# State space powers as two 64x64 blocks, and attention's value matmuls in two sets of 256 columns

## What is computed

```python
# layer 0, attention: 16 heads of 16 channels
attn = (einsum('bhqc,bhkc->bhqk', q1, k_eff1) + einsum('bhqc,bhkc->bhqk', q2, k_eff2)) * scale
attn = softmax(attn, axis=-1)
out = einsum('bhqk,bhkd->bhqd', attn, v)
...
# layer 1, state space: D_ = 256 channels, state of N_ = 16
def step(h, x_t):
    h = einsum('dnm,bdm->bdn', A, h) + Bm[None] * x_t[..., None]
    y_t = einsum('dn,bdn->bd', Cm, h) + Dm * x_t
    return (h, y_t)
_, y = scan(step, h0, swapaxes(x, 0, 1))      # x: layernormed
y = gelu(layernorm(y, ln_w, ln_b)) @ W_out.T + b_out
```

## Time and profile before

| | |
|---|---|
| median of 3 runs | 1903.34 us (1901.82 to 1905.7) |
| the profiled execution's own time | 1897.99 us |
| its span, first to last instruction | 1895.5 us |
| PE busy | 1633.4 us (86%) |
| DVE busy | 1215.1 us (64%) |
| ACT busy | 984.4 us (52%) |
| POOL busy | 431.2 us (23%) |
| mean granted TensorE clock | 0.926 |

### The profile page before, as it was taken

One profiled execution on the slowest core, in us unless ns is written; L12 is line 12 of the kernel. 1 busy time (PEld: TensorE's weight loads), 2 busy tenths in 40 slices (PEclk: granted clock), 3 DMA queues, 4 the chain that ended last, 5 costly groups with the idle time before them and its releaser, 6 DMA issues. The chain is left out here.

```text
span 1895.5 us, 33280 instructions
## 1 busy us (share of the span) xinstructions
PE 1633.4 (86%) x10504; PEld 1102.0 (58%) x10506; DVE 1215.1 (64%) x2121; ACT 984.4 (52%) x2005; POOL 431.2 (23%) x568
## 2 busy tenths in 40 slices
PE   5949999999999999988699958999888279999990
PEld 4824333333333333327588847989874169888880
DVE  6649999999999999602688686555465832222224
ACT  3412888888888888870444323434232135555442
POOL 3027000000000000000012145212122245565550
PEclk9955999999999999997799988999898589999995
DMA  5662233334443323000100021131306722222117
GB/s 194 208 176 35 41 40 53 42 52 62 56 67 41 53 41 53 19 9 17 12 1 0 1 57 46 46 89 45 90 1 200 244 87 66 66 64 66 62 65 271
DMA packets 117577, 134.55 MB, mean 71 GB/s; under 512 B 27028, under 2 KB 91560, under 8 KB 117352
## 3 DMA queue, kind: packets, MB, share of 16 engines
q1 hardware_dynamic: 104712, 107.60, 25.0%
q0 software_dynamic: 7584, 20.72, 3.4%
q10 hardware_dynamic: 5184, 4.98, 0.8%
HBM read 92.23 MB, written 36.04 MB: 68 GB/s over the span
## 5 line engine op out<-in xcount | busy, mean ns | idle before, releaser
L1845 DVE TENSOR_REDUCE mx<-ps 128x1 f32<-128x1024 f32 x512 | 602.1, 1218 | 56.7 <-PE ps L1967 56.2
L1884 ACT ACTIVATE PR<-ps 128x512 f32<-128x512 f32 x1024 | 533.1, 604 | 170.9 <-PE ps L2006 170.8
L1967 PE MATMUL ps<-KQ 48*128 48x512 f32 x1024 | 420.1, 488 | 28.5 <-PEq L238 21.7
L2006 PE MATMUL ps<-KQ 50*128 50x512 f32 x1024 | 375.2, 445 | 25.2 <-ACT PR L1884 10.7
L2006 PEld LDWEIGHTS ps<-KQ 50*128 50x128 f32 x1024 | 170.7, 185 | 329.9 <-ACT PR L1884 303.0
L1991 PE MATMUL ps<-PR,VO 128*32 128x512 f32 x2048 | 273.6, 606 | 2.1
L1967 PEld LDWEIGHTS ps<-KQ 48*128 48x128 f32 x1024 | 176.8, 196 | 80.0 <-DVE mx L1845 43.1
L1737 PEld LDWEIGHTS ps<-e_xinT,e_w 128*128 128x128 f32 x1264 | 154.8, 193 | 5.7 <-issue 1.7
L1727 PE MATMUL ps<-eW,e_hiddenT 128*128 x632 | 155.0, 388 | 3.4 <-issue 0.9
L1737 PE MATMUL ps<-e_xinT,e_w 128*128 128x128 f32 x1264 | 155.5, 277 | 1.1 <-ACT e_xinT L1669 1.1
L1697 DVE TENSOR_TENSOR e_y<-ps,b2b 128x256 f32<-128x256 f32 x79 | 33.6, 425 | 172.7 <-DMA expert_outputs<-e_y,e_y_index 163.6
(11 more groups left out here) (274 smaller groups left out, 2212.3 us busy)
## 6 DMA issues: line engine op xcount, KB each, us to landing
KQ<-qk_parts SPq DMA_DIRECT2D x192, 128.0 KB, 6.0
qk_parts<-parts SPq DMA_DIRECT2D x8, 2048.0 KB, 6.9
TB<-toeplitz_lines SPq DMA_DIRECT2D x32, 512.0 KB, 5.8
eW<-in_L_ffn_W SPq DMA_DIRECT2D x16, 512.0 KB, 6.9
eW<-in_L_ffn_W SPq DMA_DIRECT2D x8, 1024.0 KB, 12.0
e_got<-expert_outputs SPq DMA_DIRECT2D x16, 512.0 KB, 10.2
X<-in_L_attn_x SPq DMA_DIRECT2D x8, 512.0 KB, 4.8
V<-OT SPq DMA_DIRECT2D x64, 64.0 KB, 6.8
```

The costliest lines, as they stand in the source:

```text
L1845: nc.vector.tensor_reduce(mx[:, u % RING, h * QT + q:h * QT + q + 1], ps[:, b:b + 2].rearrange("p a n -> p (a n)"), AX, ALU.max, negate=Tr ...
L1884: nc.scalar.activation(PR[:, kt % 2, h], ps[:, st_bank(u, s)], ACT.Exp).then_inc(exp_done, 1)
L1967: made = nc.tensor.matmul(ps[:, max_bank(u, t) + k], kq[half(h, KROWS), 1, h % HR, q * P:(q + 1) * P], kq[half(h, KROWS), 0, h % HR, k * B ...
L2006: nc.tensor.matmul(ps[:, st_bank(u, s)], kq[half(h, AROWS), 0, h % HR, kt * P:(kt + 1) * P], kq[half(h, AROWS), 1, h % HR, qc * BANK:(qc + ...
```

## The change

In the state space stage the power is no longer kept as a 128x128 matrix with zeros off the two diagonal 64x64 blocks, but as those two blocks one above the other, 64 columns wide (`BLK`). Each former matmul of `level` becomes two of 64 rows by 64 columns: `blocks` gives the row ranges 0 to 63 and 64 to 127, and each reads and writes its own range, in the same PSUM bank. They move 64 + 2^l columns. The transposes of W1's power become matmuls with the identity, two blocks each. The last three powers go to a tile `PT` of their own, and `L1137` is split in two blocks too. DVE's and ACT's copies of the power move half as many columns. `build` uses a narrower mask. The matmuls `L1125`, `L1149`, `L1159`, `L1161`, `L1196` and `L1201` stay as they are. PE's loop over the batches is written out; the other engines keep theirs.

In attention `weigh` takes a part: part 0 moves query columns 0 to 255 for the four heads and is issued after the second block of a step, part 1 moves columns 256 to 511 after the fourth. The waits stand before part 0, the signal `pv_done` behind part 1.

```diff
-GT_, OB_, PT1_ = range(3)
-KEPT = PT1_ + len(REACH)
+GT_, OB_ = range(2)
+KEPT = 2
+BLK = P // 2
+BC = BLK // N
...
-            W1 = sbuf(s0, "W1", [P, SLOT, 2 * P])
-            W2 = sbuf(s0, "W2", [P, SLOT, 2 * P])
+            W1 = sbuf(s0, "W1", [P, SLOT, P + BLK])
+            W2 = sbuf(s0, "W2", [P, SLOT, P + BLK])
...
             KM = sbuf(s0, "KM", [P, 2, SLOT, KEPT, P])
+            PT = sbuf(s0, "PT", [P, 2, SLOT, len(REACH), BLK])
+            mask4 = sbuf(s0, "mask4", [P, BC])
...
-                    body((2 * i + 2, 0), (2 * i + 1, 1))
+                if written_out:
+                    for b in range(1, NB - 1):
+                        body((b, b % 2), (b - 1, 1 - b % 2))
+                else:
+                    with eng.Fori(0, (NB - 2) // 2) as i:
+                        body((2 * i + 1, 1), (2 * i, 0))
+                        body((2 * i + 2, 0), (2 * i + 1, 1))
...
                                             pattern=[[N, GC]], channel_multiplier=-1).then_inc(mask_ready, 1)
+                    pool.wait_ge(mask_ready, 1)
+                    nc.gpsimd.tensor_tensor(mask4[:], mask[:, 0:BC], mask[:, BC:GC], op=ALU.add).then_inc(mask_ready, 1)
...
-                        nc.vector.tensor_tensor(W1[:, :, P:2 * P].rearrange("p s (c n) -> p s c n", n=N),
-                                                vA[:, these, :].unsqueeze(2).broadcast_to([P, SLOT, GC, N]),
-                                                spread.unsqueeze(3).broadcast_to([P, SLOT, GC, N]), op=ALU.mult)
+                        nc.vector.tensor_tensor(W1[:, :, P:P + BLK].rearrange("p s (c n) -> p s c n", n=N),
+                                                vA[:, these, :].unsqueeze(2).broadcast_to([P, SLOT, BC, N]),
+                                                mask4[:].unsqueeze(1).unsqueeze(3).broadcast_to([P, SLOT, BC, N]), op=ALU.mult)
...
-                                nc.vector.tensor_copy(dst[:, :, P:2 * P], src[:, :, o:o + P]).then_inc(w1r[h], 1)
+                                nc.vector.tensor_copy(dst[:, :, P:P + BLK], src[:, :, o:o + BLK]).then_inc(w1r[h], 1)
...
-                                last = nc.scalar.copy(of_pair(KM[:, z], h)[:, :, PT1_ + l - LEVELS + 1], src[:, :, o:o + P])
+                                last = nc.scalar.copy(of_pair(PT[:, z], h)[:, :, l - LEVELS + 1], src[:, :, o:o + BLK])
                             if l <= LEVELS:
-                                last = nc.scalar.copy(dst[:, :, P:2 * P], src[:, :, o:o + P])
+                                last = nc.scalar.copy(dst[:, :, P:P + BLK], src[:, :, o:o + BLK])
...
-                                last = nc.tensor.matmul(scan(d)[:, j], KM[:, z, j, PT1_ + k], by_batch(hs[:, j:j + 1])[:, 0, :, 0:TPB - 1 - d],
-                                                        start=True, stop=True, skip_group_check=True)
+                                for r in blocks:
+                                    last = nc.tensor.matmul(scan(d)[r, j], PT[r, z, j, k], by_batch(hs[r, j:j + 1])[:, 0, :, 0:TPB - 1 - d],
+                                                            start=True, stop=True, skip_group_check=True)
...
-                                    nc.tensor.matmul(pair(0, h)[:, s % HS, 0:c + P], W2[:, s, P:2 * P], W1[:, s, P - c:2 * P], start=True, stop=True, skip_group_check=True)
-                                last = nc.tensor.matmul(pair(1, h)[:, s % HS, 0:c + P], W1[:, s, P:2 * P], W2[:, s, P - c:2 * P], start=True, stop=True, skip_group_check=True)
+                                    for r in blocks:
+                                        nc.tensor.matmul(pair(0, h)[r, s % HS, 0:c + BLK], W2[r, s, P:P + BLK], W1[r, s, P - c:P + BLK], start=True, stop=True, skip_group_check=True)
+                                for r in blocks:
+                                    last = nc.tensor.matmul(pair(1, h)[r, s % HS, 0:c + BLK], W1[r, s, P:P + BLK], W2[r, s, P - c:P + BLK], start=True, stop=True, skip_group_check=True)
...
-                                    last = nc.tensor.transpose(pair(1, h)[:, s % HS, 0:P], W1[:, s, P:2 * P], ident[:])
+                                    for r in blocks:
+                                        last = nc.tensor.matmul(pair(1, h)[r, s % HS, 0:BLK], W1[r, s, P:P + BLK], ident[r, r], start=True, stop=True, skip_group_check=True)
...
-                    batches(pe, body)
...
+    WPARTS = 2
+    PART = BANK // WPARTS
...
-            def weigh(u, step):
+            def weigh(u, step, part):
 
                 kt = step % KT
-                pe.wait_ge(exp_done, BLOCKS * u + HG * (step + 1))
-                if step == 0:
-                    pe.wait_ge(vo_ready, u + 1)
-                if kt == 0 and STEPS * u + step > 0:
-                    pe.wait_ge(ot_kept, 2 * u + step // KT)
+                if part == 0:
+                    pe.wait_ge(exp_done, BLOCKS * u + HG * (step + 1))
+                    if step == 0:
+                        pe.wait_ge(vo_ready, u + 1)
+                    if kt == 0 and STEPS * u + step > 0:
+                        pe.wait_ge(ot_kept, 2 * u + step // KT)
+                cols = slice(part * PART, (part + 1) * PART)
                 for h in range(HG):
-                    last = nc.tensor.matmul(ps[2 * HD * h:2 * HD * (h + 1), OT_BANK], VO[:, u % 2, kt, h], PR[:, kt % 2, h],
-                                            start=(kt == 0), stop=(kt == KT - 1))
-                last.then_inc(pv_done, 1)
+                    last = nc.tensor.matmul(ps[2 * HD * h:2 * HD * (h + 1), OT_BANK, cols], VO[:, u % 2, kt, h], PR[:, kt % 2, h, cols],
+                                            start=(kt == 0 and part == 0), stop=(kt == KT - 1), skip_group_check=True)
+                if part == WPARTS - 1:
...
-                    if h == HG - 1 and STEPS * u + step > 0:
-                        weigh(u if step > 0 else u - 1, (step - 1) % STEPS)
-            weigh(UNITS - 1, STEPS - 1)
+                    if h % (HG // WPARTS) == HG // WPARTS - 1 and STEPS * u + step > 0:
+                        weigh(u if step > 0 else u - 1, (step - 1) % STEPS, h // (HG // WPARTS))
+            for part in range(WPARTS):
+                weigh(UNITS - 1, STEPS - 1, part)
```

More of the change, by code:

```diff
@@ L849, in ssm @@
             slots = lambda h: range(HS * h, HS * h + HS)
+            blocks = [slice(BLK * y, BLK * (y + 1)) for y in range(P // BLK)]
             of_pair = lambda t, h: t[:, HS * h:HS * h + HS]
@@ L1214, in body @@
                             pe.wait_ge(small_kept, 2)
-                    batches(pe, body)
+                    batches(pe, body, written_out=True)
         ssm_output(nc, sem, sbuf, ps, X, Y, ident, woT, lnwb, turned)
```

9 lines of the change are left out of this document (4 added, 5 removed).

## The result

The changed kernel takes 1852.84 us (median of 4 runs, 1844.43 to 1859.64), the kernel before 1902.71 (4 runs, 1901.82 to 1905.7): a ratio of 0.9738, 95% interval 0.9708 to 0.9767. It is 50 us faster, inside the range, and 14 us slower than forecast.

What follows compares the result with a forecast made beforehand. Attention was taken as bound by PE's order, state space by PE's columns (DVE at levels 0 and 1). 1898.0 - 12 (attention) - 52 (state space) = 1834 profiled, 5.3 more for the median: 1839; range 1818 to 1858, 1872 with half overlap.

Steps and rivals of the forecast that it cites:

- the attention term: Attention: shorter steps less the copy-step wait gain 0.7 to 0.8 us in each of 16 units, 12 us.
- State space, 52 us: State space stage: seven batches gain 49 us, batch 0 gains 2, the last lone recurrence 1.
- The table: State space batch piece by piece, assuming full block overlap: 30.75 us before, 23.7 after.
- the blocks do not overlap: State space rival: blocks sharing a PSUM bank run singly; stage loses 6 us, attention gains 12: 1897 us, chance 0.08.
- Half overlap, 1864: State space rival: only some 3.5 us of the 7 per batch are gained, 1864 us, chance 0.08.
- Attention's step, 2.46: Attention: PE becomes the bound of a normal step at 2 x (0.66 + 0.57) = 2.46 us, 0.14 to 0.15 less.
- after 16 x 2.46 + 2 x 0.99 = 41.3: Attention unit after the change: sixteen steps plus two waits for ACT's copy, 41.3 us against 42.0 before.
- attention gains nothing: Attention rival: changes of layout cost 0.57 + 0.03 and more, so no gain there: 1851 us, chance 0.14.
- The stall itself: Attention, twice a unit: part 0, due at 0.66, waits 0.99 us for ACT's copy (`ot_kept`), later work queued behind.
- Without that stall it would gain 44: Attention: without the copy-step wait the stage would gain 44 us instead of 12.
- the clock falls in the batches: State space rival: PE at half the clock makes a batch 41 us, not 30.75; 1963 us, chance 0.03.
- The parts costed at nothing: PE's written-out loop, masks on POOL and narrower `build`: no cost, being behind PE's queue or before a waiting transposition.

Runs made afterwards that it cites:

- e6: Changed kernel, in each half level all matmuls of the upper 64x64 block issued first, then all of the lower: 1896.12 us (one run).
- e1: Kernel before with only attention's two half sets of value matmuls (`weigh`), old state space stage: 1903.34 us, ratio 1.0012.
- e4: Changed kernel, with both half sets behind the fourth score in the steps that wait for the copy of the heads: 1822.28 us, ratio 0.9595.
- e12: Changed kernel, both half sets behind the fourth score in unit 0 and copy steps, plus filling identity matmuls in the state space stage: 1817.51 us, ratio 0.9561.
- e7: Kernel before with only PE's loop over the batches written out: 1902.88 us, ratio 1.0006.
- e5: Changed kernel with four sets of 128 query columns, one after each score, instead of two sets: 2553.19 us (one run).
- e2: Kernel before with only the state space change (two 64x64 blocks), old attention: 1850.64 us, ratio 0.9732.
- e3: Changed kernel with ACT's copy of the heads moved ahead of its step's first exponential: 1826.04 us, ratio 0.9601.
- e11: e9 with both half sets behind the fourth score in attention unit 0: 1824.8 us, ratio 0.9607.
- e9: e3 with the copy step's first half set behind the third score instead of the second: 1828.11 us, ratio 0.9618.
- e8: Changed kernel with unread identity matmuls filling PE's gaps behind levels 1 and 2 of a batch: 1846.68 us, ratio 0.9715.
- e10: e9 with the filling identity matmuls of e8 in the state space stage: 1824.94 us, ratio 0.9599.

## Why the prediction was right, and where it was not

- **Verdict and range: right.** 1852.8 is in 1818 to 1872, and faster. The mechanisms were right. By the medians the 14 us between it and 1839 are the attention term (12) and 1.5 of the state space's. In the profiled executions the spans differ by 47.2 where 64 were forecast: 8.1 of that shortfall lie in attention, 1.4 in state space, and the other 7 in stretches that no edit touches and that differ from execution to execution.
- **State space, 52 us: right.** Alone it measured 50.5. The table gave a batch of 23.7, measured 23.97; no piece is off by more than 0.38. That one is level 8, which gained nothing: the sum had a change of layout at the taps, but not the three of 0.1 here. The seven batches gave 45.8 of their 49 (1.6 of that is the fall of the clock), batch 0 gave 2.3 for 2, the lone recurrence 2.5 for 1. Full overlap of the blocks, taken from rows of scores, maxima and L1149 beside each other, held.
- **Rival "the blocks do not overlap": wrong.** Level 3's former matmuls start 0.13 us apart, as one block's 72 columns want, and not 0.26. The rule of the Trainium skill (TensorEngine Tiling (Array Packing), Gotcha 1: PSUM Pressure), that different row tiles cannot access the same PSUM bank at once, doesn't hold for two 64x64 tiles on the diagonal of the array that write different partitions of one bank: the measurement decides. Half overlap, 1864, fell with it, and `e6` shows that PE even finds most of the overlap when the instructions stand apart.
- **Attention's step, 2.46: right to the hundredth**, in the steady step.
- **Attention's term of 12 us: mis-sized, it measured 0 by the medians and 3.9 in the profiled execution.** The failing step is "after 16 x 2.46 + 2 x 0.99 = 41.3". The stall is 1.09 and not 0.99: I let PE go on at 1.65 into the step, but the earlier trace rows have the value matmuls at 1.75, 0.15 behind the copy's end, so I read that start as free of the wait and it was not. That is 0.2 us a unit. The sum had no place for DVE's row work while DVE is behind, 0.22 a unit. Together 41.75 and not 41.3: 0.42 x 16 = 7 us. Then 12 was too much for its own terms: 14 x 2.605 + 2 x 2.75 is 41.97 and the other side 41.34, 0.63 a unit, 10 us. The gain left, some 0.25 x 15 = 4 us in the steady units, stands in the changed kernel's stage (672.9 to 669.0); in `e1` the late rise of the clock in the first unit takes back 47.11 - 44.37 = 2.7 of it. Where these 4 us go in the medians, no trace shows. So the rival "attention gains nothing", 1851, is what the medians say, and for another reason than it named: the changes of layout in attention cost just what I took for them.
- **The stall itself: right in place and cause.** "Without that stall it would gain 44" was too much: `e4`, without the stall but with two old-order copy steps of 2.75 in a unit, gained 31 over the changed kernel, and `e12`, with its other two edits, 35.
- **Rival "the clock falls in the batches": real but small.** In one steady batch of the changed kernel the granted clock was 0.50 from 1222.3 to 1225.8, and it cost 25.58 - 23.97 = 1.6 us, not 17 per batch. PE's timeline there; level 3's starts are 0.24 us apart where they were 0.13, level 4's last ones are back at 0.14:

```profile
1222.38 0.51 PE L1186 MATMUL ps<-W 64*64 64x72 f32 x4
1222.62 0.51 PE L1188 MATMUL ps<-W 64*64 64x72 f32 x4
...
1225.89 0.33 PE L1188 MATMUL ps<-W 64*64 64x80 f32 x4
1226.03 0.33 PE L1186 MATMUL ps<-W 64*64 64x80 f32 x4
```

- **What I did not look for** is the clock at attention's start. The trace of before had it: the stage begins at 0.50 for 8.6 us. A change that alters what PE runs there may move that moment, and no term of the sum asked for it. In the changed kernel's own profile it cost nothing (9.7 us, a first unit of 44.28).
- **The parts costed at nothing:** the written-out loop is shown to be free (`e7`). POOL's masks and the narrower `build` were not tried apart.

## What to carry to other kernels

When a set of work is split to give its consumers a finer grain, each wait that stood in front of the whole set moves forward with the first part: look up what the wait is for and keep the old order in the steps where it isn't covered (here 2 of 16 steps, worth 31 us). When the wait ends is read from the start of what waited, not from the end of what it waited for: here 0.15 lay between them. A unit's sum needs the engine that is nearest to full, too: DVE had 0.1 us of slack per step, so after each stall its small extra work came out on PE's path. And small square tiles on the diagonal are worth trying for block-diagonal operands, since here the columns saved were saved in full; each change between such tiles and undivided matmuls seems to have taken back about 0.1 us.

## What the runs showed of the hardware

- Two 64x64 matmuls with rows and columns 0 to 63 and 64 to 127, both into one PSUM bank, run side by side: eight pairs of 72 columns in 1.03 us, against 1.94 for eight undivided matmuls of 136. A block alone takes 0.06 us a record (`e6`), and no more with the other beside it.
- Where 64x64 blocks and undivided matmuls meet, PE took 0.09 to 0.10 us more each time (three places behind level 7 of one batch; no run tests it alone).
- Records of matmuls in different blocks start out of program order: in `e6` those of the scan between those of the level ahead of it.
- The granted clock can stay at half with PE busy all the time. At the start of attention it rose 8.6 to 13.5 us after the first score with the old order in the first unit (five profiled executions), 9.4 to 31.7 with the new one (eight), and with four sets of 128 columns (`e5`, one) not for 1376 us. That the order causes this isn't shown: an execution of the kernel before had a mean clock of 0.553 over 2630 us.
- Which order is faster depends on the clock: a step of attention takes 2.60 us in the old order and 2.46 in the new one at the full clock, 4.07 and 4.32 at half of it.
- A fall of the clock in a steady batch lasted 3.4 us and cost 1.6. It came, 7 us into one batch, in the profiled executions of the changed kernel, `e2`, `e3`, `e4` and `e11` (there in the last batch), not in those of `e5` and `e9`, nor in the three with filled gaps (`e8`, `e10`, `e12`). `e6`, whose batches are longer, had a fall in several in a row.
